# Self-attention of a Perceiver layer: projections and scores issued in groups of two head pairs, the loads around them rearranged

## Chip, cores, metric

The kernel runs on one core of a Trainium2 chip. Its time is the device time of one launch in microseconds (us), here the median of three runs of the kernel before. Beside it stands one execution that the hardware profiler recorded; all durations in this document that are not called the median come from that execution.

## Reference

One layer in fp32 on x, of shape (2, 256, 256), with a context of (2, 4096, 256). It has three parts, each added to x after a layer norm of x: cross-attention on the context, self-attention with 16 heads of 64 channels and 16 learnt memory keys ahead of the 256 token keys, and a gated FFN with quantised weights. The change touches self-attention alone:

```python
q = x @ Wq
k, v = jnp.split(x @ Wkv, 2, axis=-1)             # 16 heads of 64, memory keys and values ahead
dots = jnp.einsum('bhid,bhjd->bhij', q, k) * scale
dots = jnp.einsum('bhij,hk->bkij', dots, pre_proj)   # heads are mixed before the softmax
dots = jnp.where(causal, mask_value, dots)
attn = jax.nn.softmax(dots, axis=-1)
attn = jnp.einsum('bhij,hk->bkij', attn, post_proj)  # and after it
out = jnp.einsum('bhij,bhjd->bhid', attn, v)
out = out.transpose(0, 2, 1, 3).reshape(b, n, INNER) @ Wo
```

## The kernel before

Three functions follow one another, each a block that starts all engines together: cross-attention (to about 1103 us of the span), `self_attention` (to about 1290 us), and the FFN. Each engine runs its own list of instructions in order; semaphores tie them together, and every order in it is written out by hand.

`self_attention` begins with the layer norm of x. VectorE takes the statistics of four token tiles (`normalise_rows`, L56 and L60), GpSimd turns the variances into inverse deviations (`invert_std`, L71 to L75), VectorE scales (L64), TensorE transposes the result (L1249) and VectorE copies it to `xnT` (L1125). GpSimd has other work in the same stretch, ahead of `invert_std` in its list: it clears the padded `xnT` (L985) and makes the constants `spread` and `columns` (L986 to L995).

SyncE issues all loads of this part: the queries' weights (L963), the keys' and values' weights as one load of 2 MB (L964), the two mixing matrices (L965, L966), eight small loads of the memory keys (L968), three FFN weights (L769), the output weights (L972). After them it issues, with GpSimd, the regrouping of the scores (L956), copies from SBUF to SBUF that bring the heads of a row of queries together.

TensorE then projects. A projection (`project`, L1289) is two products of 128x128 weights with 512 columns, four matmul passes in fp32. The 26 projections are Q and K of pair 0, Q and K of pair 1, and so on for eight pairs of heads (n = 0 to 15), then ten for V (n = 16 to 25). Projection n writes one of four half banks (banks 2 and 3), and waits until projection n - 4 was copied out: even n by ScalarE (L1053), odd n by VectorE (L1020, L1024). Scores (`dots`, L1300) of a pair are four passes on 64 rows of the array, two for each head; step n of `dots` writes bank n % 2 and waits until step n - 2 was copied out (ScalarE L1056 for even n, VectorE L1166 for odd n). Steps 0 to 7 are the first 128 queries (144 keys), 8 to 15 the second 128 queries (272 keys) of batch item 0. The order is: projections 2m and 2m + 1, then dots m - 1, for m = 0 to 7; dots 7; then dots 8 + n and V projection n in turn, for n = 0 to 7; then the last two V projections. Between projections 2 and 3 TensorE makes the small constants (`small_constants`, L1257 and L1259: one product with `spread`, one transpose of the memory keys) and waits until VectorE copied them (L1135).

VectorE's copy of each odd projection is followed by one of six parts of the quantisation of an FFN weight (`quantise_weight`, L780 to L800); the first copy of a projection on VectorE waits for the three FFN weights (`hidden_in`). After the projections come the transposes of the FFN weights (L807), then the mixing steps (L1315), the softmax, the product with V and the output.

Of the kernel before, what the change touches and what calls it, by code (L numbers as in the profile page):

```python
# [12 lines left out]
P = 128  # L13
# [3 lines left out]
INNER = HEADS * DH  # L17
TOK_TILES = BATCH * SEQ // P
QT = SEQ // P
DC = D // P  # L20
PAIRS = HEADS // 2
# [47 lines left out]
def invert_std(pool, moments, power, chain, inverse_std):  # L69

    pool.memset(power[:, :], -0.5).then_inc(inverse_std, 1)  # L71
    pool.wait_ge(chain, 2 * TOK_TILES)
    pool.tensor_scalar(moments[:, :, 1], moments[:, :, 1], EPS, None, ALU.add).then_inc(inverse_std, 1)
    pool.wait_ge(inverse_std, 2)
    pool.tensor_tensor(moments[:, :, 1], moments[:, :, 1], power[:, :], ALU.pow).then_inc(inverse_std, 1)  # L75
# [665 lines left out]
MEM = 16  # L741
# [68 lines left out]
def self_attention(nc, w_q, w_kv, w_o, pre_proj, post_proj, mem_k, mem_v, w_gate, w_up, w_down, ffn_wT,  # L810
# [9 lines left out]
    with ExitStack() as stack:  # L820
        r = Resources(nc, stack)
# [21 lines left out]
        moments = r.sbuf("moments2", [P, TOK_TILES, 2])  # L843
# [24 lines left out]
        bank = [r.psum(f"bank{n}", [P, 2, 512]) for n in range(4)]  # L868

        wq_in = r.sem("wq_in")  # L870
        wkv_in = r.sem("wkv_in")
        wo_in = r.sem("wo_in")
        hidden_in = r.sem("hidden_in")
        hidden_chain = r.sem("hidden_chain")
# [39 lines left out]
        NQK = 2 * PAIRS  # L914
# [46 lines left out]
        @block.sync  # L961
        def _(sp):
            sp.dma_start(wq_sb, w_q.rearrange("(c p) n -> p c n", p=P)).then_inc(wq_in, 16)  # L963
            sp.dma_start(wkv_sb, w_kv.rearrange("(c p) n -> p c n", p=P)).then_inc(wkv_in, 16)  # L964
            sp.dma_start(proj_sb[:, 0, :], pre_proj).then_inc(small_in, 16)  # L965
            sp.dma_start(proj_sb[:, 1, :], post_proj).then_inc(small_in, 16)  # L966
            for pair in range(PAIRS):
                sp.dma_start(memk_sb[pair * MEM:(pair + 1) * MEM, :, :],  # L968
                             mem_k[2 * pair:2 * pair + 2].rearrange("h m d -> m h d")).then_inc(small_in, 16)
            for n, w in ((GATE, w_gate), (UP, w_up), (DOWN, w_down)):  # L970
                load_ffn_weight(sp, hidden_w[n], w, hidden_in)
            sp.dma_start(wo_sb[:, :, :], w_o.rearrange("(c p) n -> p c n", p=P)).then_inc(wo_in, 16)  # L972
            for b in range(BATCH):
                for t in range(QT):
                    regroup(sp, b, t, 0)
                if b == 0:
                    for eng in range(2):
                        sp.wait_ge(proj_copied[eng], NPROJ // 2)
                    for m in range(BATCH):
                        sp.dma_start(v_sb[0:MEM, m * QT, :].rearrange("m (h d) -> m h d", h=HEADS),  # L980
                                     mem_v.rearrange("h m d -> m h d")).then_inc(memv_in, 16)

        @block.gpsimd
        def _(pool):
            pool.memset(xnT[:, :, :], 0.0).then_inc(padded, 1)  # L985
            pool.memset(spread[:, :], 1.0).then_inc(consts, 1)  # L986
            for n in range(GPS):
                for c in range(STEP_ROWS):
                    pool.memset(columns[:, n, c:c + 1], float(c - n * ROWS)).then_inc(consts, 1)
            pool.wait_ge(consts, 1 + GPS * STEP_ROWS)  # L990

            pool.affine_select(out=spread[:, :], in_=spread[:, :], compare_op=ALU.is_ge, fill=0.0, base=0,
                               pattern=[[1, P]], channel_multiplier=-ROWS).then_inc(consts, 1)
            pool.wait_ge(consts, 2 + GPS * STEP_ROWS)
            pool.affine_select(out=spread[:, :], in_=spread[:, :], compare_op=ALU.is_ge, fill=0.0, base=ROWS - 1,  # L995
                               pattern=[[-1, P]], channel_multiplier=ROWS).then_inc(consts, 1)
            invert_std(pool, moments, power, norm_chain, inverse_std)

            for b in range(BATCH):
                if b > 0:  # L1000
                    for t in range(QT):
                        regroup(pool, b, t, 1)
                for s in range(RING):
                    n = b * SA_STEPS + s
                    if n >= RING:
                        pool.wait_ge(post_made, n - RING + 1)
                    pool.memset(expd[:, n % RING, :, step_keys(s):KEYS], 0.0).then_inc(tail_zero, 1)
                if b == 0:
                    for t in range(QT):
                        regroup(pool, b, t, 1)  # L1010
# [16 lines left out]
        def copy_dots(eng, scaled_copy, n):  # L1027
            t = n // PAIRS % QT
            pair = n % PAIRS
            keys = dot_keys(t)  # L1030
            eng.wait_ge(dots_made, n + 1)
            if n >= PAIRS:

                for half in range(2):
                    eng.wait_ge(regrouped[half][pair], 16 * (n // PAIRS))
            scaled_copy(dots_sb[:, 2 * pair:2 * pair + 2, 0:keys], bank[n % 2][:, :, 0:keys]
                        ).then_inc(dots_copied[n % 2], 1)
# [13 lines left out]
        def _(act):  # L1051
# [6 lines left out]
            def copy_projections(first, end):  # L1058
                for n in range(first, end, 2):
                    act.wait_ge(proj_made, n + 1)  # L1060
                    copy_projection(copy, n)
# [17 lines left out]
                for n in range((b * QT + t) * PAIRS, (b * QT + t + 1) * PAIRS, 2):  # L1079
                    copy_dots(act, scaled_copy, n)  # L1080

            for m in range(PAIRS):
                copy_projections(2 * m, 2 * m + 2)
                if m > 0 and (m - 1) % 2 == 0:
                    copy_dots(act, scaled_copy, m - 1)
            if (PAIRS - 1) % 2 == 0:
                copy_dots(act, scaled_copy, PAIRS - 1)
            for n in range(PAIRS, 2 * PAIRS):
                if n % 2 == 0:
                    copy_dots(act, scaled_copy, n)  # L1090
# [29 lines left out]
        def _(dve):  # L1120
# [84 lines left out]
                for n in range((b * QT + t) * PAIRS + 1, (b * QT + t + 1) * PAIRS, 2):  # L1205
                    copy_dots(dve, scaled_copy, n)

            for m in range(PAIRS):
                copy_projections(2 * m, 2 * m + 2)
                if m > 0 and (m - 1) % 2 == 1:  # L1210
                    copy_dots(dve, scaled_copy, m - 1)
            if (PAIRS - 1) % 2 == 1:
                copy_dots(dve, scaled_copy, PAIRS - 1)
            for n in range(PAIRS, 2 * PAIRS):
                if n % 2 == 1:
                    copy_dots(dve, scaled_copy, n)
# [27 lines left out]
        def _(pe):  # L1244
            mm = pe.matmul
            pe.wait_ge(norm_chain, NORMALISED)
            for c in range(DC):
                for t in range(TOK_TILES):
                    last = pe.transpose(bank[0][:, c, t * P:(t + 1) * P], xn[:, t, c * P:(c + 1) * P], ident[:, :])  # L1249
                last.then_inc(xT_made, 1)  # L1250
            pe.wait_ge(xT_copied, DC)
            pe.wait_ge(wq_in, 16)

            def small_constants():
                pe.wait_ge(small_in, 16 * (2 + PAIRS))
# [3 lines left out]
                pe.transpose(bank[1][:, 1, 0:P], memk_sb[:, :, :].rearrange("p a d -> p (a d)"), ident[:, :]  # L1259
                             ).then_inc(memk_made, 1)  # L1260

            def project(n):
                kind, m = projections[n]
                if n == 1:
                    pe.wait_ge(wkv_in, 16)
                if n == 3:
                    small_constants()
                    pe.wait_ge(memk_copied, BATCH)
                if n >= 4:
                    pe.wait_ge(proj_copied[n % 2], (n - 4) // 2 + 1)  # L1270
                for c in range(DC):
                    if kind == Q:
                        w, a = wq_sb[:, c, m * P:(m + 1) * P], xnT_tokens[:, c]
                    elif kind == K:
                        w, a = wkv_sb[:, c, m * P:(m + 1) * P], xnT_tokens[:, c]
                    else:
                        at = INNER + (m % 2) * 512
                        first = m // 2 // QT * PADDED + m // 2 % QT * P
                        a = wkv_sb[:, c, at:at + 512]
                        if m < 2 * TOK_TILES:  # L1280
                            w = xnT[:, c, first:first + P]
                        else:
                            w = [xnT[:, c, b * PADDED + QT * P:b * PADDED + QT * P + TAIL_ROWS] for b in range(BATCH)]
                    if kind == V and m >= 2 * TOK_TILES:
                        for b in range(BATCH):
                            last = mm(projection_bank(n)[b * TAIL_ROWS:(b + 1) * TAIL_ROWS], w[b], a,
                                      start=(c == 0), stop=(c == DC - 1))
                    else:
                        last = mm(projection_bank(n), w, a, start=(c == 0), stop=(c == DC - 1))  # L1289
                last.then_inc(proj_made, 1)  # L1290
# [71 lines left out]
            def dots_of_pair(m):  # L1362
                for eng in range(2):
                    pe.wait_ge(proj_copied[eng], m + 1)
                dots(m)

            for m in range(PAIRS):
                project(2 * m)
                project(2 * m + 1)
                if m > 0:  # L1370
                    dots_of_pair(m - 1)
            dots_of_pair(PAIRS - 1)
            for n in range(PAIRS):
                dots(PAIRS + n)
                project(NQK + n)
            for n in range(NQK + PAIRS, NPROJ):
                project(n)
            for eng in range(2):
# [378 lines left out]
```

## Time and profile before

| | us |
|---|---|
| median of 3 runs | 1374.15 (1373.31 to 1375.81) |
| the profiled execution | 1373.69 |
| its span | 1371.9 |
| TensorE busy | 1266.9 |
| VectorE busy | 865.2 |
| ScalarE busy | 880.6 |
| GpSimd busy | 411.3 |

The span is what the engines' records cover; 1.8 us of the execution's time lie around it. Times on the left of a row of the timeline are counted from the span's start. PE is the matmul engine (TensorE), PEld its weight loads, DVE VectorE, ACT ScalarE, POOL GpSimd, SP SyncE; a q behind an engine's name means its queue (sequencer), which issues DMAs. The time in brackets is how long the engine had been idle, with what ended it.

### The profile page before, as it was taken

How to read it: one execution, taken by the hardware profiler on the slowest of the kernel's cores; microseconds unless marked ns; L12 is line 12 of the kernel's file. 1: busy time of each engine (PE TensorE's matmuls, PEld its weight loads, DVE VectorE, ACT ScalarE, POOL GpSimd, SP SyncE). 2: the span in 40 equal slices, each digit the busy share in tenths (PEclk: the TensorE clock that was granted, in tenths of full speed). 3: DMA queues.
4: the chain of work that ended last, by engine and by line, in shares of the span. 5: the costliest groups of instructions: out<-in, count | busy, mean ns of one | idle time of the engine just before them, and what ended most of it. 6: DMA issues, size and time to landing. Idle time of an engine off the chain costs nothing. (4 is left out here: it accounts for less than half of the span.)

```text
span 1371.9 us, 21416 instructions
## 1 busy us (share of the span) xinstructions
PE 1266.9 (92%) x8447; PEld 1004.7 (73%) x8447; DVE 865.2 (63%) x1121; ACT 880.6 (64%) x1543; POOL 411.3 (30%) x373
## 2 busy tenths in 40 slices
PE   4999999999999999999999999999999969898663
PEld 3887887878787878697878787878887734667422
DVE  4547575766766576736766766576757645657366
ACT  5858586867777776766867777776868412535242
POOL 4506061524334342321524334242515022030000
PEclk9999999999999999999999999999999979998876
DMA  5000000000000011200000000000000063352000
GB/s 172 1 2 20 1 20 1 20 1 20 11 10 16 1 36 47 81 1 1 20 0 20 14 8 20 1 20 2 16 1 4 1 202 58 38 68 33 1 0 16
DMA packets 29683, 34.62 MB, mean 25 GB/s; under 512 B 3984, under 2 KB 26000, under 8 KB 29328
## 3 DMA queue, kind: packets, MB, share of 16 engines
q1 hardware_dynamic: 27536, 29.83, 8.4%
q0 software_dynamic: 2048, 3.43, 1.8%
q8 instruction: 68, 1.11, 0.4%
q14 instruction: 31, 0.25, 0.1%
HBM read 25.89 MB, written 0.52 MB: 19 GB/s over the span
## 5 line engine op out<-in xcount | busy, mean ns | idle before, releaser
L505 DVE TENSOR_TENSOR prob_sum<-prob_sum,probs 128x1024 f32<-128x1024 f32 x224 | 261.7, 1222 | 171.0 <-ACT probs L426 170.3
L341 POOL TENSOR_TENSOR k_split<-probs,k_split 64x512 fp32r<-64x512 f32 x128 | 164.5, 1285 | 359.0 <-ACT probs L388 357.5
L482 DVE TENSOR_REDUCE step_max<-scores_a 128x2 f32<-128x1024 f32 x128 | 156.7, 1224 | 96.7 <-PE scores_a L608 96.7
L343 POOL TENSOR_TENSOR k_split<-probs,k_split 64x512 fp32r<-64x512 f32 x128 | 164.6, 1286 | 9.6
L426 ACT ACTIVATE probs<-scores_a 128x1024 f32<-128x1024 f32 x98 | 100.5, 1026 | 93.8 <-PE scores_a L621 93.8
L482 DVE TENSOR_REDUCE step_max<-scores_b 128x2 f32<-128x1024 f32 x128 | 155.7, 1217 | 0.0
L426 ACT ACTIVATE probs<-scores_b 128x1024 f32<-128x1024 f32 x98 | 100.6, 1027 | 55.9 <-PE scores_b L621 55.9
L333 POOL TENSOR_TENSOR w_lo<-w_raw,w_hi 128x768 fp32r<-128x768 f32 x16 | 38.4, 2400 | 298.3 <-ACT w_hi L355 298.2
L632 PE MATMUL out_ps<-probs,v_far 128*64 128x256 f32 x1024 | 118.0, 382 | 0.0
L632 PE MATMUL out_ps<-probs,v_near 128*64 128x256 f32 x1024 | 118.0, 382 | 0.0
L620 PE MATMUL scores_a<-q_twice,k_split 128*128 128x256 f32 x392 | 100.3, 288 | 0.2 <-ACT probs L426 0.2
L620 PE MATMUL scores_b<-q_twice,k_split 128*128 128x256 f32 x392 | 99.8, 287 | 0.0
L621 PE MATMUL scores_b<-q_low_max,k_ones 128*128 128x256 f32 x392 | 98.0, 282 | 0.0
L621 PE MATMUL scores_a<-q_low_max,k_ones 128*128 128x256 f32 x392 | 97.8, 282 | 0.0
L632 PEld LDWEIGHTS out_ps<-probs,v_near 128*64 128x64 f32 x1024 | 70.5, 137 | 36.8 <-issue 0.4
L632 PEld LDWEIGHTS out_ps<-probs,v_far 128*64 128x64 f32 x1024 | 70.5, 137 | 36.6
L572 PE MATMUL k_both<-ctxT_lo,w_hi 128*128 128x512 f32 x256 | 90.3, 434 | 5.6 <-ACT probs L388 3.5
L608 PE MATMUL scores_b<-k_split,q_twice 128*128 128x512 f32 x256 | 84.8, 413 | 8.4 <-DVE step_max L482 6.9
L379 ACT ACTIVATE k_split<-k_both 64x512 fp32r<-64x512 f32 x128 | 75.4, 589 | 20.9 <-PE k_both L572 19.4
L426 ACT ACTIVATE probs<-k_both 128x1024 f32<-128x1024 f32 x60 | 61.6, 1026 | 39.5 <-PE k_both L621 39.5
L403 ACT ACTIVATE k_ones<-k_split 64x512 fp32r<-64x512 f32 x128 | 80.7, 631 | 2.8
L405 ACT ACTIVATE k_ones<-k_split 64x512 fp32r<-64x512 f32 x128 | 80.4, 628 | 3.1
(218 smaller groups left out, 2866.0 us busy)
## 6 DMA issues: line engine op xcount, KB each, us to landing
ctx_rows<-in_ctx_dram SPq DMA_DIRECT2D x10, 512.0 KB, 3.9
w_raw<-in_L_xattn_w_v_dram SPq DMA_DIRECT2D x14, 256.0 KB, 3.4
probs<-in_ctx_dram SPq DMA_DIRECT2D x6, 512.0 KB, 6.2
grouped<-dots_sb SPq DMA_DIRECT2D x16, 136.0 KB
grouped<-dots_sb POOLq DMA_DIRECT2D x16, 136.0 KB, 13.2
w_raw<-in_L_xattn_w_q_dram SPq DMA_DIRECT2D x16, 128.0 KB, 2.4
w_raw<-in_L_xattn_w_k_dram SPq DMA_DIRECT2D x16, 128.0 KB, 2.6
wo_pair<-in_L_xattn_w_o_dram SPq DMA_DIRECT2D x16, 128.0 KB, 2.1
```

Of the source, the lines that this page charges most:

```text
L341: pool.tensor_tensor(k_split[DH:P, A, keys], staged[0:DH], k_split[0:DH, A, keys].bitcast(F32), ALU.subtract).then_inc(k_low, 1)
L343: pool.tensor_tensor(k_split[0:DH, B, keys], staged[DH:P], k_split[DH:P, B, keys].bitcast(F32), ALU.subtract).then_inc(k_low, 1)
L403: act.activation(k_ones[0:DH, A, keys], k_split[0:DH, A, keys].bitcast(F32), ACT.Copy).then_inc(k_copied, 1)
L405: act.activation(k_ones[DH:P, B, keys], k_split[DH:P, B, keys].bitcast(F32), ACT.Copy).then_inc(k_copied, 1)
L426: act.activation(probs[:, j % 2, h, :], flat_scores[score_bank(b, i, 2 * j + h)], ACT.Exp, scale=SCALE).then_inc(exp_done, 1)
L482: dve.tensor_reduce(step_max[:, :, 1 - h, j - 1], scores[h][:, :, :], X, ALU.max).then_inc(max_done, 1)
L505: dve.tensor_tensor(prob_sum[:, h, :], prob_sum[:, h, :], probs[:, j % 2, h, :], ALU.add).then_inc(sum_done, 1)
L572: last = mm(k_ps[j % 2][:, :], w[:, c, 0:PAIR], s[:, c, j * CHUNK:(j + 1) * CHUNK], start=(n == 0), stop=(n == len(passes) - 1))
L608: last = mm(scores[h][:, qt, :], q_twice[:, h, qt * P:(qt + 1) * P], k_split[:, h, keys], start=True, stop=True)
L620: mm(out, k_split[:, h, keys], q_twice[:, h, :], start=True, stop=False)
L621: last = mm(out, k_ones[:, h, keys], q_low_max[:, h, :], start=False, stop=True)
L632: last = mm(out_ps[h * DH:(h + 1) * DH, SEQ:2 * SEQ], v[:, h * DH:(h + 1) * DH], probs[:, j % 2, h, t * SEQ:(t + 1) * SEQ], start=(j == 0 ...
```

## The change

The order of projections and dots goes from one pair at a time to two: four projections, then two dots. For the first half it is projections 0 to 3, 4 to 7, dots 0 and 1, projections 8 to 11, dots 2 and 3, projections 12 to 15, dots 4 and 5, dots 6 and 7; then dots 8 and 9, V projections 0 and 1, and so on. The copies on ScalarE and VectorE follow that order in the first half. The keys' and values' weights come as two loads of 1 MB on semaphores of their own. The ten small loads (mixing matrices, memory keys) are issued by ScalarE. GpSimd runs `invert_std` directly after clearing `xnT`. TensorE makes the small constants directly after the transposes of x, ahead of its waits for `xT_copied` and `wq_in`.

```diff
--- before.py
+++ after.py
@@ -868,7 +868,7 @@
         bank = [r.psum(f"bank{n}", [P, 2, 512]) for n in range(4)]
 
         wq_in = r.sem("wq_in")
-        wkv_in = r.sem("wkv_in")
+        wkv_in = [r.sem("wk_in"), r.sem("wv_in")]
         wo_in = r.sem("wo_in")
         hidden_in = r.sem("hidden_in")
         hidden_chain = r.sem("hidden_chain")
@@ -961,12 +961,10 @@
         @block.sync
         def _(sp):
             sp.dma_start(wq_sb, w_q.rearrange("(c p) n -> p c n", p=P)).then_inc(wq_in, 16)
-            sp.dma_start(wkv_sb, w_kv.rearrange("(c p) n -> p c n", p=P)).then_inc(wkv_in, 16)
-            sp.dma_start(proj_sb[:, 0, :], pre_proj).then_inc(small_in, 16)
-            sp.dma_start(proj_sb[:, 1, :], post_proj).then_inc(small_in, 16)
-            for pair in range(PAIRS):
-                sp.dma_start(memk_sb[pair * MEM:(pair + 1) * MEM, :, :],
-                             mem_k[2 * pair:2 * pair + 2].rearrange("h m d -> m h d")).then_inc(small_in, 16)
+            for part in range(2):
+                columns_of = slice(part * INNER, (part + 1) * INNER)
+                sp.dma_start(wkv_sb[:, :, columns_of], w_kv[:, columns_of].rearrange("(c p) n -> p c n", p=P)
+                             ).then_inc(wkv_in[part], 16)
             for n, w in ((GATE, w_gate), (UP, w_up), (DOWN, w_down)):
                 load_ffn_weight(sp, hidden_w[n], w, hidden_in)
             sp.dma_start(wo_sb[:, :, :], w_o.rearrange("(c p) n -> p c n", p=P)).then_inc(wo_in, 16)
@@ -983,6 +981,8 @@
         @block.gpsimd
         def _(pool):
             pool.memset(xnT[:, :, :], 0.0).then_inc(padded, 1)
+            invert_std(pool, moments, power, norm_chain, inverse_std)
+            pool.wait_ge(inverse_std, 3)
             pool.memset(spread[:, :], 1.0).then_inc(consts, 1)
             for n in range(GPS):
                 for c in range(STEP_ROWS):
@@ -994,7 +994,6 @@
             pool.wait_ge(consts, 2 + GPS * STEP_ROWS)
             pool.affine_select(out=spread[:, :], in_=spread[:, :], compare_op=ALU.is_ge, fill=0.0, base=ROWS - 1,
                                pattern=[[-1, P]], channel_multiplier=ROWS).then_inc(consts, 1)
-            invert_std(pool, moments, power, norm_chain, inverse_std)
 
             for b in range(BATCH):
                 if b > 0:
@@ -1079,12 +1078,16 @@
                 for n in range((b * QT + t) * PAIRS, (b * QT + t + 1) * PAIRS, 2):
                     copy_dots(act, scaled_copy, n)
 
-            for m in range(PAIRS):
-                copy_projections(2 * m, 2 * m + 2)
-                if m > 0 and (m - 1) % 2 == 0:
-                    copy_dots(act, scaled_copy, m - 1)
-            if (PAIRS - 1) % 2 == 0:
-                copy_dots(act, scaled_copy, PAIRS - 1)
+            act.dma_start(proj_sb[:, 0, :], pre_proj).then_inc(small_in, 16)
+            act.dma_start(proj_sb[:, 1, :], post_proj).then_inc(small_in, 16)
+            for pair in range(PAIRS):
+                act.dma_start(memk_sb[pair * MEM:(pair + 1) * MEM, :, :],
+                              mem_k[2 * pair:2 * pair + 2].rearrange("h m d -> m h d")).then_inc(small_in, 16)
+            for m in range(0, PAIRS, 2):
+                copy_projections(2 * m, 2 * m + 4)
+                if m > 0:
+                    copy_dots(act, scaled_copy, m - 2)
+            copy_dots(act, scaled_copy, PAIRS - 2)
             for n in range(PAIRS, 2 * PAIRS):
                 if n % 2 == 0:
                     copy_dots(act, scaled_copy, n)
@@ -1205,12 +1208,11 @@
                 for n in range((b * QT + t) * PAIRS + 1, (b * QT + t + 1) * PAIRS, 2):
                     copy_dots(dve, scaled_copy, n)
 
-            for m in range(PAIRS):
-                copy_projections(2 * m, 2 * m + 2)
-                if m > 0 and (m - 1) % 2 == 1:
+            for m in range(0, PAIRS, 2):
+                copy_projections(2 * m, 2 * m + 4)
+                if m > 0:
                     copy_dots(dve, scaled_copy, m - 1)
-            if (PAIRS - 1) % 2 == 1:
-                copy_dots(dve, scaled_copy, PAIRS - 1)
+            copy_dots(dve, scaled_copy, PAIRS - 1)
             for n in range(PAIRS, 2 * PAIRS):
                 if n % 2 == 1:
                     copy_dots(dve, scaled_copy, n)
@@ -1248,8 +1250,6 @@
                 for t in range(TOK_TILES):
                     last = pe.transpose(bank[0][:, c, t * P:(t + 1) * P], xn[:, t, c * P:(c + 1) * P], ident[:, :])
                 last.then_inc(xT_made, 1)
-            pe.wait_ge(xT_copied, DC)
-            pe.wait_ge(wq_in, 16)
 
             def small_constants():
                 pe.wait_ge(small_in, 16 * (2 + PAIRS))
@@ -1259,12 +1259,17 @@
                 pe.transpose(bank[1][:, 1, 0:P], memk_sb[:, :, :].rearrange("p a d -> p (a d)"), ident[:, :]
                              ).then_inc(memk_made, 1)
 
+            small_constants()
+            pe.wait_ge(xT_copied, DC)
+            pe.wait_ge(wq_in, 16)
+
             def project(n):
                 kind, m = projections[n]
                 if n == 1:
-                    pe.wait_ge(wkv_in, 16)
+                    pe.wait_ge(wkv_in[0], 16)
+                if n == NQK:
+                    pe.wait_ge(wkv_in[1], 16)
                 if n == 3:
-                    small_constants()
                     pe.wait_ge(memk_copied, BATCH)
                 if n >= 4:
                     pe.wait_ge(proj_copied[n % 2], (n - 4) // 2 + 1)
@@ -1364,15 +1369,19 @@
                     pe.wait_ge(proj_copied[eng], m + 1)
                 dots(m)
 
-            for m in range(PAIRS):
-                project(2 * m)
-                project(2 * m + 1)
+            for m in range(0, PAIRS, 2):
+                for n in range(2 * m, 2 * m + 4):
+                    project(n)
                 if m > 0:
+                    dots_of_pair(m - 2)
                     dots_of_pair(m - 1)
+            dots_of_pair(PAIRS - 2)
             dots_of_pair(PAIRS - 1)
-            for n in range(PAIRS):
+            for n in range(0, PAIRS, 2):
                 dots(PAIRS + n)
+                dots(PAIRS + n + 1)
                 project(NQK + n)
+                project(NQK + n + 1)
             for n in range(NQK + PAIRS, NPROJ):
                 project(n)
             for eng in range(2):
```

## Rows read from the trace of the kernel before

**Rows 1.** The page, busy time by engine.

```profile
PE 1266.9 (92%) x8447; PEld 1004.7 (73%) x8447; DVE 865.2 (63%) x1121; ACT 880.6 (64%) x1543; POOL 411.3 (30%) x373
```

**Rows 2.** Windows: sum; PE, PEld, DVE, ACT, POOL busy; granted clock, DMA share, GB/s.

```profile
1103.00:1110.00 7.00, 0.01 (x1) 0.02 (x1) 4.10 (x12) 0.00 (x0) 5.32 (x42) 0.50 0.80 300
...
1122.00:1148.00 26.00, 26.00 (x76) 11.02 (x76) 17.43 (x25) 7.46 (x9) 3.92 (x6) 1.00 0.18 46
```

**Rows 3.** Timeline from 1103 us, GpSimd and VectorE: start, duration, what.

```profile
1103.27 1.04 POOL L985 MEMSET xnT<- 128x1120 f32 x1 [42.55 <-POOLq L95]
...
1104.75 0.38 DVE L60 BATCH_NORM_AGGREGATE moments<-stats 128x2 f32<-128x6 f32 x4
...
1106.23 0.22 POOL L73 TENSOR_SCALAR moments<-moments 128x4 f32<-128x4 f32 x1
1106.53 1.05 POOL L75 TENSOR_TENSOR moments<-moments,power 128x4 f32<-128x4 f32 x1
...
1107.61 2.32 DVE L64 TENSOR_SCALAR normed<-x_res,moments 128x256 f32<-128x256 f32 x4 [2.48 <-POOL moments L75]
```

**Rows 4.** Timeline of PE, first projections and the small constants.

```profile
1109.98 1.97 PE L1249 MATMUL bank<-ident,normed 128*128 128x128 f32 x8 [7.73 <-DVE normed L64]
1112.74 7.99 PE L1289 MATMUL bank<-xnT,shared 128*128 128x512 f32 x12 [0.78 <-DVE xnT L1125]
1120.66 0.40 PE L1257 MATMUL bank<-proj_sb,spread 16*128 16x32 f32 x2
...
1121.91 1.98 PE L1289 MATMUL bank<-xnT,shared 128*128 128x512 f32 x4 [0.58 <-DVE kT L1135]
```

**Rows 5.** Timeline, projections and dots in turn, with two weight loads.

```profile
1127.90 0.52 PE L1300 MATMUL bank<-kT,q_sb 64*128 64x144 f32 x4
...
1129.31 0.19 PEld L1289 LDWEIGHTS bank<-xnT,shared 128*128 128x128 f32 x1 [0.24 <-issue]
...
1129.74 0.19 PEld L1289 LDWEIGHTS bank<-xnT,shared 128*128 128x128 f32 x1 [0.24 <-issue]
...
1131.98 0.52 PE L1300 MATMUL bank<-kT,q_sb 64*128 64x144 f32 x4
...
1152.00 0.73 PE L1300 MATMUL bank<-kT,q_sb 64*128 64x272 f32 x4
...
1154.58 0.73 PE L1300 MATMUL bank<-kT,q_sb 64*128 64x272 f32 x4
```

**Rows 6.** Timeline around dots 6, 7 and 8, PE and VectorE.

```profile
1148.28 0.52 PE L1300 MATMUL bank<-kT,q_sb 64*128 64x144 f32 x4
...
1149.00 1.74 DVE L782 TENSOR_REDUCE w_scales<-wide 128x48 f32<-128x1536 f32 x1
...
1150.09 1.99 PE L1289 MATMUL bank<-shared,xnT 128*128 128x512 f32 x4
...
1150.66 0.45 DVE L1166 TENSOR_SCALAR dots_sb<-bank 128x288 f32<-128x288 f32 x1
```

**Rows 7.** SyncE's issues on the timeline: start, time that issuing took.

```profile
1105.24 3.73 SPq L968 DMA_DIRECT2D memk_sb<-in_L_attn_mem_k_dram  x8
...
1110.11 3.44 SPq L769 DMA_DIRECT2D wide<-in_L_ffn_w_down_dram  x1
```

**Rows 8.** DMA issues by line: count, KB each, us from issue to landing.

```profile
wo_pair<-in_L_xattn_w_o_dram SPq DMA_DIRECT2D x16, 128.0 KB, 2.1
...
shared<-in_L_attn_Wkv_dram SPq DMA_DIRECT2D x1, 2048.0 KB, 10.2
...
wide<-in_L_ffn_w_down_dram SPq DMA_DIRECT2D x1, 768.0 KB, 12.2
memk_sb<-in_L_attn_mem_k_dram SPq DMA_DIRECT2D x8, 8.0 KB, 7.7
```

**Rows 9.** Windows in the first mixing steps, columns as in rows 2.

```profile
1178.00:1182.00 4.00, 2.53 (x20) 2.38 (x20) 2.69 (x15) 1.81 (x12) 0.00 (x0) 1.00 0.56 62
...
1182.80:1186.20 3.40, 3.40 (x18) 3.35 (x17) 2.46 (x12) 2.03 (x10) 0.00 (x0) 0.50 0.01 1
```

## The prediction

> **What bounds the kernel now.** The page comes first: TensorE is busy for 92% of the span [rows 1]. The change lies in the 70 us at the start of self-attention, so the windows of that stretch come next. They show two regimes. From 1103 to 1110 us TensorE has nothing to do and its clock is granted at 0.50 (1.2 GHz), while VectorE and GpSimd work on the layer norm; from 1122 to 1148 us TensorE is busy all the time at 1.00 (2.4 GHz) [rows 2]. So the first regime is a chain through VectorE and GpSimd, and in the second only work or turns taken from TensorE itself count. I then read the timeline for what ends each wait. VectorE is idle for 2.48 us before L64, and GpSimd's power (L75) ends it [rows 3]. TensorE is idle for 7.73 us before the transposes, ended by L64; for 0.78 us before the first projection, ended by the copy of xnT; and projection 3 starts only after the small constants were copied, ended by L1135 [rows 4]. Whatever comes later in the kernel waits for this stretch, since the mixing starts after the last projection; a microsecond saved here is a microsecond of the span.
>
> **Part 1: GpSimd's deviation first.** L73 needs VectorE's aggregates, done at 1104.75 + 0.38 = 1105.13, yet it starts at 1106.23, since the constants stand ahead of it in GpSimd's list [rows 3]. Afterwards only the clearing of xnT (to 1104.31) and one small memset are ahead, so L73 starts at about 1105.20: **1.03 us earlier**, and L75, L64 and the transposes with it. The constants move behind L75. They filled GpSimd from 1104.31 to 1106.23, 1.92 us; from about 1106.6 on they end at 1108.6. Who needs them is the small-constants product, now at 1110.9 (below): cover 2.3 us. Behind them GpSimd has memsets of expd and the regrouping, whose first piece waits for dots.
>
> **Part 2: small constants ahead of the wait for xT.** Now L1257 starts at 1120.66, and the next projection at 1121.91 [rows 4]. Without them it would start at 1120.66: **1.25 us off**. They move to the end of the transposes, where TensorE idles for 0.78 us anyway. L1257 alone takes 0.40 us and both less than 1.25 us; at the lower clock of that stretch they may stick out of the 0.78 us. Bounds: 0 and 0.5 us; I take 0.1, since the two lie nearer to 0.7 us than to 1.25. Net 1.15. The copy by VectorE, for which projection 3 waits, is then done about 8 us before it is asked for.
>
> **Part 3: fewer turns between projections and dots.** One projection pass starts every 0.43 us (1129.31 to 1129.74); a pair with its dots takes 1131.98 - 1127.90 = 4.08 us, eight passes 3.44, leaving 0.64 for dots of 144 keys. With 272 keys: 2.58 - 4 x 0.43 = 0.86 [rows 5]. Four passes of 272 columns at 0.43 x 272/512 would alone take 0.91, so the two heads must overlap on their halves of the array: 0.46 and 0.24 us for the two sizes. Both leave the same rest, **0.40 us, for turning from 128 rows to 64 and back**. Before, there are 14 such turns (dots 0 to 5 singly, 6 to 8 together, 9 to 15 singly); afterwards 6: {0,1}, {2,3}, {4 to 9}, {10,11}, {12,13}, {14,15}. 8 x 0.40 = **3.2 us off**. If a turn is paid per dots and not per change, nothing is saved; if all of the rest goes, 3.2. I take 3.2 as the two sizes agree on it.
>
> **Part 4: what the grouping adds in the middle.** Dots 4 to 9 now stand in a row, on two banks. Call T the end of projection 15. VectorE's list is: copy K of pair 7, then a part of the quantisation (L782), and only then the copy of dots 5. In the trace of before L782 starts 0.72 us after T = 1148.28 and takes 1.74, so the copy behind it starts at T + 2.38 and takes 0.45 [rows 6]. Dots 7 wait for that copy, to T + 2.9. Dots 9 need dots 7 copied (0.52 for their passes by the record of dots 6, 0.45 for the copy, and what signalling adds): T + 4.0, then 0.46 and 0.2 for turning back: V projection 0 at T + 4.65. Pure work is 4 x 0.24 + 2 x 0.46 + 0.40 = 2.28, so TensorE stalls for 2.37. Before, T to the first V projection is 1150.09 - 1148.28 = 1.81 [rows 6] against 1.34 of work, a stall of 0.47. **Net 1.9 us on**. Late next would be ScalarE's copy of dots 6, which is ready 1 us before anyone waits.
>
> **Edits at nothing, and their cover.** SyncE loses ten issues (eight took 3.73 us, 0.47 each [rows 7]) and gains one; the FFN loads start up to 4 us earlier, but bytes are the limit: the DMA share is 0.80 from 1103 to 1110 [rows 2]. The last FFN weight lands at 1110.11 + 12.2 = 1122.3 [rows 7, 8]. VectorE's first K copy waits for it, and TensorE asks for that copy (projection 5) at about 1123.0: up to 0.2 us of stall if it lands no earlier; I put 0. The keys' weights land no later than the 2 MB did, at about 1113.9, when projection 1 needs them two microseconds or more later; the values' weights are not used before 1148. ScalarE's ten issues end at 1103.3 + 10 x 0.47 = 1108.0, and its first copy comes after 1115. Their landing is the unknown cost.
>
> **When do the small loads land?** TensorE asks for them at the end of the transposes, 1111.95 - 1.03 = 1110.9. No load of before was issued by ScalarE. Lower bound: the short load nearest to it took 2.1 us [rows 8], 1108.0 + 2.1 = 1110.1. Upper bound: the same loads on SyncE's queue, behind 3 MB of weights, took 7.7 us [rows 8], 1115.7. I take the lower end, since the 7.7 us were spent behind transfers of the same queue, and the small loads now share it with none. The Trainium skill, page "DMA: Bandwidth & Descriptors", section "Queues, rings and completion order", says that an engine of the DMA serves its queues in turn, a packet at a time. By that rule they would land little after the lower end and the sum would stand; by the row of SyncE's queue it would come to 1.9 us slower. No row of before has two such queues under full load.
>
> **Sum:** -1.03 - 1.15 - 3.2 + 1.9 = -3.5 us. Against the profiled execution (1373.69) that is 1370.2; it lies 0.46 under the median of 1374.15, so the forecast is **1370.6**. Bounds: -4.9 (the middle stall half of what I work out, small terms at their better end) to -2.6.
>
> **Rivals.**
>
> **A. The small loads land late (slower).** The place is TensorE's wait ahead of the first projection. Each microsecond after 1110.9 is one on the span, and the 0.6 us of constants lose their cover. The gain is gone at 1110.9 + 2.9 = 1113.8, and slower by over 0.2% from about 1116.6. At the 7.7 us of rows 8 it is +1.9 (1376.0). If ScalarE's issue is held as SyncE's was for 3.44 us at L769 [rows 7], the last landing is 1108.0 + 3.44 + 7.7 = 1119.1, 8.2 us late: -3.5 + 8.2 + 0.6 = +5.3, **1379.4**. For it: small loads among saturated engines; against it: their own queue. The Trainium skill, page "DMA: Bandwidth & Descriptors", section "Queues, rings and completion order", adds that ScalarE's queue is not a descriptor generator of its own. By that rule a full backlog of SyncE's could hold the small ones; no row here shows it either way.
>
> **B. They land 1 to 3 us late.** Then the gain shrinks to 0.4 to 2 us: about **1372.7**.
>
> **C. The clock falls in the middle.** Part 4 leaves TensorE idle for some 2 us between sparse dots. In the first mixing steps, where it was busy for 2.53 of 4 us with short passes, the clock fell to 0.50 for 3.4 us afterwards [rows 9]. The same behind T would cost half of 3.4 us, 1.7: **1372.3**; twice that, 1374.0. Against it: the stall stands between two dense stretches.
>
> **D. The turns cost per dots.** Then part 3 is void: -0.3, **1373.9**. Against it: equal rests of two sizes.
>
> **Chances.** Forecast 0.45; A at over 0.2% slower 0.10; A short of that and B 0.18; C 0.22; D 0.05. 0.2% is 2.75 us, about what a measurement of this kernel can tell from no change. Faster by more: the forecast and a few of the others, 0.48; within: B, C, D and most of what A has left, 0.42; slower 0.10. The range runs from 1369.0 to 1375.5; it leaves out the worse half of A and little below.
>
> **What would show it.** L73 at about 1105.2 and L1249 at 1109.0; L1257 directly behind the transposes, and the first projection at 1111.8 (A, B: later, with an idle time before L1257); no gap before projection 3; four passes at 0.43 between turns and a pair of dots of 272 keys with its turn at 1.3 us; dots 7 starting 2.9 us after dots 4, behind L782 and L1166; granted clock 1.00 through that stretch (C: 0.50); mixing 3.5 us earlier. The forecast is wrong if the first projection starts later than at 1112.7, or if the period of two V projections with two dots stays at 5.15 us instead of 4.75.

## The result, and the profile after

The median of 20 runs is 1378.17 us, against 1374.49 us for the kernel before in as many runs: a ratio of 1.0024, with a 95% interval of 1.0014 to 1.0035. The change makes the kernel slower by some 3.3 us; I had forecast 3.5 us off. A second measurement of the same kernel gave 1.0010 (0.9994 to 1.0026). The second interval still includes no change, so the loss rests on the first measurement and on the stage below.

Spans alone mislead here. The profiled execution of the changed kernel has a span of 1376.8 us, 4.9 more than before, but 2.42 of them lie ahead of self-attention, in code that did not change: the stage starts at 1105.69 us instead of 1103.27. Over the fourteen profiled executions of this study that start lies anywhere between 1101.6 and 1106.5 us, for the kernel before at 1103.27 and 1104.67, for the changed one at 1105.69 and 1103.38. So I read the **stage** instead: from GpSimd's clearing of xnT to the first mixing pass, 74.97 us before (twice) and 77.39 us changed (76.60 in its second profile). Behind the stage the two traces run alike: 193.66 us to the end of the span before, 193.72 changed. This part too varies from one execution to the next, between 192.6 and 195.6 us over the fourteen (192.6 in the second profile of the kernel before). The stage's 2.4 us are what the change costs; the rest of the 3.3 lies within the interval.

The start of the stage, in the changed kernel's timeline (GpSimd, VectorE, TensorE, ScalarE's and SyncE's queues):

```profile
1105.69 1.04 POOL L983 MEMSET xnT<- 128x1120 f32 x1 [42.57 <-POOLq L95]
...
1106.61 4.35 ACTq L1084 DMA_DIRECT2D memk_sb<-in_L_attn_mem_k_dram  x8
...
1107.64 0.23 POOL L73 TENSOR_SCALAR moments<-moments 128x4 f32<-128x4 f32 x1 [0.87 <-DVE moments L60]
...
1109.03 3.53 DVE L64 TENSOR_SCALAR normed<-x_res,moments 128x256 f32<-128x256 f32 x4 [1.48 <-POOL moments L75]
1109.05 0.19 POOL L986 MEMSET spread<- 16x128 f32 x1
1109.20 1.21 POOL L989 MEMSET columns<- 128x1 f32 x32
1110.03 5.27 SPq L769 DMA_DIRECT2D wide<-in_L_ffn_w_down_dram  x1
...
1111.13 1.28 POOL L1006 MEMSET expd<- 128x480 f32 x3
...
1112.62 1.97 PE L1251 MATMUL bank<-ident,normed 128*128 128x128 f32 x8 [7.93 <-DVE normed L64]
...
1118.51 0.63 PE L1257 MATMUL bank<-proj_sb,spread 16*128 16x32 f32 x2 [3.92 <-DMA memk_sb<-in_L_attn_mem_k_dram]
1119.07 0.47 PE L1259 MATMUL bank<-ident,memk_sb 128*128 128x128 f32 x1
...
1119.34 10.95 PE L1294 MATMUL bank<-xnT,shared 128*128 128x512 f32 x20
```

Three things are to be seen, with the times of before in [rows 3, 4]. L73 runs 1.01 us earlier in the stage (1.95 instead of 2.96 us in), as forecast. L64 behind it takes 3.53 us instead of 2.32, with two runs of GpSimd's memsets beside it, the small ones of `columns` and then the three of expd, so that the transposes start 6.93 us in instead of 6.71: later, not earlier. And TensorE then stands for 3.92 us for the last load of the memory keys. The first projection starts 13.65 us in instead of 9.47: **4.18 us late**.

The middle of the stage, in PE's timeline of the changed kernel:

```profile
1150.87 0.76 PE L1305 MATMUL bank<-kT,q_sb 64*128 64x144 f32 x8
1151.99 0.52 PE L1305 MATMUL bank<-kT,q_sb 64*128 64x144 f32 x4 [0.36 <-ACT dots_sb L1055]
1153.84 2.34 PE L1305 MATMUL bank<-kT,q_sb 64*128 64x144 f32 x12 [1.33 <-DVE dots_sb L1169]
1156.12 4.57 PE L1294 MATMUL bank<-shared,xnT 128*128 128x512 f32 x8
1160.61 1.19 PE L1305 MATMUL bank<-kT,q_sb 64*128 64x272 f32 x8
...
1165.36 1.19 PE L1305 MATMUL bank<-kT,q_sb 64*128 64x272 f32 x8
```

and its windows (columns as in rows 2):

```profile
1151.00:1154.70 3.70, 2.01 (x20) 1.33 (x20) 3.00 (x4) 0.82 (x2) 1.31 (x3) 0.97 0.21 40
...
1154.50:1157.85 3.35, 3.35 (x10) 1.34 (x7) 1.08 (x2) 0.62 (x1) 2.45 (x5) 0.50 0.70 104
1157.95:1160.00 2.05, 2.05 (x6) 0.94 (x5) 0.00 (x0) 0.60 (x1) 0.00 (x0) 1.00 0.66 73
```

Dots 4 start at T = 1150.87, dots 7 at T + 2.97 (forecast 2.9), the first V projection at T + 5.25 (forecast 4.65). The clock fell to 0.50 for 3.4 us behind the stall: rival C happened as well. Two V projections with two dots take 1165.36 - 1160.61 = 4.75 us, as forecast.

### The profile page after: what moved, and what is told of

The parts are those of the page before. It is cut to its first block and busy times, and to the rows that moved or that the text cites. A ratio compares the mean times of both kernels' runs of the same rounds, so it can differ in the third digit from the quotient of the medians.

```text
span 1376.8 us, 21418 instructions
## 1 busy us (share of the span) xinstructions
PE 1267.8 (92%) x8447; PEld 1010.6 (73%) x8447; DVE 866.5 (63%) x1121; ACT 879.8 (64%) x1543; POOL 411.5 (30%) x373
```

## The experiments

Names with b_ are the kernel before with one part of the change; names with a_ are the changed kernel with one part undone. In the table, transposes and first projection are starts in us into the stage; the last two columns are lengths in us.

| kernel | ratio to before (95%) | transposes | first projection | first projection to last two V | stage |
|---|---|---|---|---|---|
| before | 1 | 6.71 | 9.47 | 57.28 | 74.97 |
| changed | 1.0024 (1.0014 to 1.0035) | 6.93 | 13.65 | 55.52 | 77.39 |
| changed, again | 1.0010 (0.9994 to 1.0026) | 6.93 | 12.10 | 56.28 | 76.60 |
| a_consts_back | 1.0001 (0.9987 to 1.0015) | 6.93 | 9.68 | 56.13 | 74.03 |
| a_sp_waits | 1.0025 (1.0011 to 1.0039) | 6.93 | 9.68 | 58.91 | 76.81 |
| b_act_loads | 1.0006 (0.9992 to 1.0019) | 6.73 | 9.48 | 57.10 | 74.80 |
| b_dev_first | 0.9989 (0.9978 to 1.0001) | 6.93 | 9.68 | 56.21 | 74.11 |
| b_dev_quiet | 0.9992 (0.9979 to 1.0006) | 4.78 | 7.53 | 58.32 | 74.07 |
| b_consts_late | 1.0000 (0.9987 to 1.0014) | 6.72 | 9.47 | 56.58 | 74.28 |
| b_group | 0.9986 (0.9975 to 0.9997) | 6.73 | 9.48 | 56.79 | 74.50 |
| b_group_mid | 0.9984 (0.9971 to 0.9997) | 6.73 | 9.48 | 54.22 | 71.92 |
| best1 | 0.9963 (0.9949 to 0.9978) | 4.78 | 7.53 | 54.46 | 70.21 |
| best2 | 0.9954 (0.9938 to 0.9970) | 4.77 | 7.52 | 54.01 | 69.75 |

One caution on the last two columns: the clock rises from 0.50 to 1.00 between 3.1 and 5.5 us after the first projection (5.2 before), and differs in this also between kernels that do the same there. A microsecond earlier is half a microsecond of stage, so a stage length is good to about 1 us. The starts ahead of it repeat to 0.02 us where no load is awaited.

**The early wait for the small loads: a_consts_back.**

```diff
-            small_constants()
             pe.wait_ge(xT_copied, DC)
...
                 if n == 3:
+                    small_constants()
                     pe.wait_ge(memk_copied, BATCH)
```

> The changed kernel with the small constants back between projections 2 and 3. Stage time is counted from the clearing of xnT to the first mixing pass: 74.97 us before, 77.39 changed. If the early wait for the small loads is the cause (theory 1), the first projection starts about 9.7 us into the stage instead of 13.65, the 1.3 us gap at projection 3 is back, and the stage takes 77.39 - 4.0 + 1.3 - 0.8 (constants no longer ahead) = about 74.0. If the order in groups or the middle stall costs the time (theory 2), the stage stays near 77.

The first projection starts 9.68 us in, and the stage takes 74.03: theory 1. The stage is 3.4 us shorter than the changed kernel's, and the measured loss is gone (1.0001). Not all of the 3.4 is the place of that one wait. The start is 3.97 us earlier and the gap at projection 3 is back, at 1.25 us, which leaves 2.7 for the wait. The rest is the clock, which did not fall in the middle here (some 1.5) and rose 1.0 us later behind the first projection (0.5 the other way). The three make 3.7, good to the 1 us said above. What is left against before is 0.22 us on for L64 and 1.3 off by parts 3 and 4: 73.9 by the sum.

**Why the loads come late: b_act_loads and a_sp_waits.** The first moves the ten loads to ScalarE in the kernel before and nothing else.

> The kernel before with the ten small loads issued by ScalarE and nothing else. They landed 12.8 us into the stage in the changed kernel. If two queues under full load are the cause, they land at about the same time here (12 to 13 us), no engine waits for them (asked for at 17.4 us), and the stage stays at 75.0, or 74.8 if the FFN weights land earlier. If they landed late because of something else in the change, they land at about 7 us.

The second holds SyncE's queue back in the changed kernel:

```diff
             sp.dma_start(wq_sb, ...).then_inc(wq_in, 16)
+            sp.wait_ge(small_in, 16 * (2 + PAIRS))
             for part in range(2):
```

> The changed kernel, but SyncE issues the keys' and all later weights only after the small loads have landed, so that the small loads share the DMA engines with 1 MB alone. If the backlog of SyncE's queue makes them late, they land about 2 us after the last issue, 7.3 to 7.5 us into the stage, and the first projection starts at about 9.8 instead of 13.65. If ScalarE's issues are slow by themselves, they land later than 10. The FFN weights land 2 us later (about 21), which may stall projection 5: stage 74 to 76.

The DMA issues of the memory keys (the last figure of a row is the median time from issue to landing), first of the changed kernel:

```profile
memk_sb<-in_L_attn_mem_k_dram ACTq DMA_DIRECT2D x8, 8.0 KB, 6.3
```

then of a_sp_waits:

```profile
memk_sb<-in_L_attn_mem_k_dram ACTq DMA_DIRECT2D x8, 8.0 KB, 3.3
```

A load of 8 KB on ScalarE's queue lands after 6.3 us beside SyncE's backlog and after 3.3 us with only the queries' weights in flight; the latest of the eight took 8.0 and 4.3. SyncE could go on 7.07 us into the stage, so the small loads had landed by then instead of at 12.8, and the first projection came at 9.68. In b_act_loads the eight took 6.3 to 7.2 us with the other parts of the change absent. So it is the backlog, and not the position of ScalarE's issues or anything else in the change. Where between issue and landing the small loads are held, no run here separates. The price of the cure was as high as the illness: the FFN weights came later, TensorE stood 0.40 us for the keys' weights and 2.70 us for the first K copy, the clock fell behind that gap, and the kernel is as slow as the changed one (1.0025).

The Trainium skill says in "DMA: Bandwidth & Descriptors", section "Issuing engines are not separate DMA queues", that issuing from several engines saves no more than the sequencer's time for issuing. The runs agree in the main: on SyncE's queue the eight took 7.7 us to land [rows 8], on ScalarE's 6.3, and not the 2.1 that I had hoped for from a queue of their own.

**GpSimd beside VectorE: b_dev_first and b_dev_quiet.** Both put `invert_std` first in the kernel before; they differ in one wait of GpSimd ahead of the constants:

```diff
             invert_std(pool, moments, power, norm_chain, inverse_std)
-            pool.wait_ge(inverse_std, 3)
+            pool.wait_ge(norm_chain, NORMALISED)
             pool.memset(spread[:, :], 1.0).then_inc(consts, 1)
```

> The kernel before with the deviation first on GpSimd and nothing else. My forecast was 1.03 us off. Theory 3, from the changed kernel's trace (L64 3.53 us instead of 2.32, with GpSimd's small memsets beside it): the power ends 1.0 us earlier, but L64 takes about 3.5 us, and the transposes start 0.2 us later; stage 75.0 to 75.2. If the longer L64 has another cause (the loads of ScalarE), L64 stays at 2.3 and the stage takes 74.0.

> As b_dev_first, but GpSimd starts the constants only when L64 is done. Theory 3: L64 takes 4 x 0.4 = 1.6 us, the transposes start 5.0 us into the stage instead of 6.71, the stage takes about 73.3. If GpSimd's work beside L64 is not what makes it long, L64 takes 2.3 to 3.5 us as in b_dev_first.

L64 in the two, by its line (durations of one in ns: shortest, median, longest); first b_dev_first:

```profile
L64 DVE TENSOR_SCALAR normed<-x_res,moments x4: 396/867/1641, 1106.8 to 1108.7; 128x256 f32<-128x256 f32 x4
```

then two of its four one by one, the first and the last:

```profile
L64 DVE TENSOR_SCALAR normed<-x_res,moments x1: 1332/1332/1332, 1106.8 to 1106.8; 128x256 f32<-128x256 f32 x1
...
L64 DVE TENSOR_SCALAR normed<-x_res,moments x1: 1641/1641/1641, 1108.7 to 1108.7; 128x256 f32<-128x256 f32 x1
```

GpSimd beside them, in the same execution:

```profile
1107.00 1.21 POOL L991 MEMSET columns<- 128x1 f32 x32
...
1108.93 1.28 POOL L1008 MEMSET expd<- 128x480 f32 x3
```

and L64 in b_dev_quiet:

```profile
L64 DVE TENSOR_SCALAR normed<-x_res,moments x4: 408/409/413, 1109.1 to 1110.1; 128x256 f32<-128x256 f32 x4
```

Each of the four takes 0.41 us when GpSimd is silent. In b_dev_first the first takes 1.33 us and is done at about 1108.2, as the 32 memsets of 128x1 end; the next two take 0.40 each, beside two selects on 16 partitions; the last takes 1.64 us, and ends at 1110.36, 0.15 us behind the three memsets of expd. So two of the four are held, each until a whole run of memsets is over. The row of before (2.32 us in all, [rows 3]) was itself a contended one: there the first alone is held, for 1.36 us beside expd's memsets, and the other three take 0.40. The 1.21 us more are a second run beside L64, the small memsets that moved (0.9), and 0.3 more beside expd's. Silence brings the transposes 1.93 us forward, from 6.71 to 4.78. The ScalarE loads have no part in it: with them alone, in b_act_loads, L64 takes 2.32 us. A kernel with the small memsets alone beside L64 was not tried. The Trainium skill says in "SBUF — State Buffer", section "Who interferes with whom", that VectorE in its two-port mode and GpSimd hold a port pair for a whole instruction and exclude one another. The trace agrees with the exclusion, though none of these runs shows the mode of L64; but one of expd's memsets lasts 0.44 to 0.49 us and a small one 0.10, and the instructions beside them lost 1.23 and 0.92 us, so each lost more than one turn.

b_dev_first has its transposes 0.22 us late, as theory 3 had it; its stage is a microsecond shorter than expected all the same, since the clock rose 3.1 us after the first projection there instead of 5.2.

In b_dev_quiet the 1.93 us did not reach the end of the stage: it takes 74.07. PE's timeline of b_dev_quiet at the first dots, and VectorE's:

```profile
1121.95 1.98 PE L1290 MATMUL bank<-xnT,shared 128*128 128x512 f32 x4 [0.58 <-DVE kT L1136]
1125.46 0.52 PE L1301 MATMUL bank<-kT,q_sb 64*128 64x144 f32 x4 [1.52 <-DVE kT L1021]
```

```profile
1124.62 0.69 DVE L1021 COPY kT<-bank 128x512 f32<-128x512 f32 x1 [1.77 <-DMA wide<-in_L_ffn_w_down_dram]
```

VectorE stands in front of its first copy of K for the last FFN weight, and TensorE behind it for 1.52 us. The weights land some 19 us into the stage, whatever starts earlier; they are next in line.

**The constants without the wait for their copy: b_consts_late.** The wait for `memk_copied` moves from projection 3 to the first dots.

> The kernel before, with the small constants still ahead of projection 3, but the wait for their copy only at the first dots. If the wait for the copy is a good part of the 1.25 us of part 2, projection 3 starts 0.6 us sooner behind L1257 and the stage loses 0.6; if the FFN weights (19 us into the stage) bind behind it, the gain appears as a wait for the K copy and the stage stays at 74.5 to 75.

Projection 3 follows L1257 after 0.51 us instead of 1.25, so 0.74 of the 1.25 us was waiting. PE's timeline:

```profile
1118.51 0.40 PE L1257 MATMUL bank<-proj_sb,spread 16*128 16x32 f32 x2
1118.84 0.34 PE L1259 MATMUL bank<-ident,memk_sb 128*128 128x128 f32 x1
1119.02 1.88 PE L1288 MATMUL bank<-xnT,shared 128*128 128x512 f32 x4
1121.62 0.52 PE L1299 MATMUL bank<-kT,q_sb 64*128 64x144 f32 x4 [0.73 <-DVE kT L1020]
```

The next wait takes it back: 0.73 us ahead of the first dots, for VectorE's first copy of K. That copy starts 19.0 us into the stage, where the last FFN weight lands. The ratio of 1.0000 says so too. The stage of 74.28 is 0.7 shorter because the clock rose 1.3 us earlier.

**The grouping: b_group and b_group_mid.** b_group has the order and the copies of the change and nothing else. b_group_mid lets VectorE copy dots 5, 7 and 9 ahead of a part of the quantisation (the loops that copied them later leave them out, which is not shown):

```diff
                     copy_projection(dve.tensor_copy, n)
+                    if dots_between and n == NQK - 1:
+                        copy_dots(dve, scaled_copy, PAIRS - 3)
+                        copy_dots(dve, scaled_copy, PAIRS - 1)
+                        copy_dots(dve, scaled_copy, PAIRS + 1)
                     m, part = n // 2 // W_PARTS, n // 2 % W_PARTS
```

> The kernel before with the grouping alone. By parts 3 and 4 of the prediction: 3.2 us off, 1.9 us on in the middle, stage 73.6; with a fall of the clock in the middle as in the changed kernel (granted 0.50 for 2.9 us) up to 1.5 more, 75.1. If turns are paid per dots (rival D), 76.9.

> Grouping alone, and VectorE copies dots 5, 7 and 9 directly after the last K, ahead of the part of the quantisation. If that part is what stalls the middle, dots 7 start 1.3 us after dots 4 instead of 2.97, the first V projection 3.1 us after them instead of 5.25, the clock stays at 1.00, and the stage is 2 to 3 us shorter than b_group.

b_group is faster than before (0.9986). Its stage, 74.50, lies between the forecast with and without a fall of the clock, and the clock did fall, for 3.4 us, which the eight passes behind the stall show (5.40 us instead of 3.70); against that it rose 1.9 us earlier behind the first projection, worth 0.9. PE's timeline of b_group_mid in the middle:

```profile
1149.09 0.76 PE L1302 MATMUL bank<-kT,q_sb 64*128 64x144 f32 x8
1150.21 0.81 PE L1302 MATMUL bank<-kT,q_sb 64*128 64x144 f32 x8 [0.36 <-ACT dots_sb L1056]
1151.23 1.19 PE L1302 MATMUL bank<-kT,q_sb 64*128 64x272 f32 x8 [0.20 <-ACT dots_sb L1056]
1152.34 3.70 PE L1291 MATMUL bank<-shared,xnT 128*128 128x512 f32 x8
```

The V projections start 3.25 us after dots 4, instead of 4.70 in b_group and 5.25 in the changed kernel; the first eight of their passes take 3.70 us instead of 5.40 and 4.57, and the clock stays at 1.00. From the first projection to the last two V the kernel needs 54.22 us instead of 57.28, 3.06 off. The sum of it: 3.2 us of part 3, less 0.5, since the middle still stalls for 3.25 - 2.28 = 0.97 us instead of 0.47, and 0.4 for a clock that rose 4.5 us after the first projection instead of 5.2. The total agrees within its interval: 0.9984 is 2.2 us (0.4 to 4.0).

**Together: best1 and best2.** best1 is b_dev_quiet, b_group_mid and b_consts_late in one, with all loads on SyncE's queue as before. best2 also moves the wait for the FFN weights:

```diff
-            dve.wait_ge(hidden_in, 48)
...
                     copy_projection(dve.tensor_copy, n)
+                    if n == 1:
+                        dve.wait_ge(hidden_in, 48)
```

> All that is expected to help: deviation first with the constants after L64 (1.7 us off), grouping with the dots' copies ahead of the quantisation (3 to 4 off), small constants made ahead of projection 3 with the wait for their copy only at the first dots (0.7 off); loads as before on SyncE. Stage 69 to 70 us, time about 1369.

> best1, but VectorE waits for the FFN weights behind its first copy of K instead of ahead of it. In best1 and b_dev_quiet the earlier start ran into the landing of the last FFN weight, 19 us into the stage (TensorE idle 1.52 us for the K copy in b_dev_quiet). If that is what kept b_dev_quiet from its full gain, no such gap is left and the stage takes 68.5 to 69.2 us instead of 70.21; if another wait ends there, it stays at 70.

best1 gave 1369.61 us, 0.9963; best2 1368.81 us, 0.9954, or 6.3 us less than before. In best2 no idle time stands between the first projection and the first dots any more; its stage of 69.75 missed the 69.2 that I expected, with no new wait to be seen there. The step from best1 to best2 is 0.46 us of stage. The clock rises at nearly the same point in both (5.5 and 5.4 us after the first projection), and the twenty passes ahead of the first dots take 9.16 us in best1 and 8.75 in best2. In best1 VectorE still waited there, 1.35 us, for the last FFN weight. So the traces, one of each, show that wait at 0.4 us. The totals can't tell the two kernels apart; that both beat before and changed they show.

**Both kernels once more: a_again and b_again.**

> The changed kernel once more, for how far its stretches repeat. Expected: small loads landed 12.5 to 13 us into the stage, first projection at 13.3 to 13.9, dots 7 at 3.0 us behind dots 4; stage 76 to 78, as the clock's rise and its fall in the middle shift by up to 2 us.

> The kernel before once more. Expected: first projection 9.47 us into the stage, stage 74 to 75.5. The start of the stage moves with the cross-attention ahead of it, which took 1103.27 us before and 1105.69 in the changed kernel: if that difference is chance and none of the change's, this run starts anywhere between 1101 and 1107.

The kernel before repeats in the starts of the table to 0.02 us. The changed kernel does not: TensorE waited 2.37 us for the loads instead of 3.92, and started projecting at 12.10 instead of 13.65, which is below the 13.3 that I had expected at least. So this wait on loads among saturated engines differed by 1.5 us between two executions. The clock fell in the middle again.

## Why the prediction was wrong

**Part 1 (1.03 off) failed in its last link.** L73 and L75 came earlier as worked out. I moved L64 along with them at its 2.32 us, and costed the constants behind L75 by asking only who needs them (cover 2.3 us), not what runs beside them. Beside them ran L64, at 3.53 us, since the moved memsets held its first instruction for 0.9 us and expd's still held its last. The transposes were 0.22 us later instead of 1.03 earlier (b_dev_first alone gives the same 0.22).

**The landing of the small loads (taken at 1110.1) is the step that turned the sign.** I put it at the lower end, by loads of 128 KB (2.1 us in the median) from a stretch without such a backlog, and took the 7.7 us of SyncE's queue for the effect of a shared queue. They landed at about 1105.69 + 12.8, which counted from the old start is 1116.1: my upper end was 1115.7, and rival A the right case, at a chance of 0.28 in its two forms with B. The landing alone would have stayed just short of rival A's 1116.6 for a loss of over 0.2%; L64 and the clock made up the rest. Its mechanism, ScalarE's issue held, was at most a small part: the eight issues took 4.35 us instead of 3.73. The rule of taking turns that I cited from the Trainium skill ("DMA: Bandwidth & Descriptors", "Queues, rings and completion order") did not give the early landing that I read into it.

**Part 2 (1.15 off)** did take away the gap: the projections run from 0 to 7 without one. It was paid for with the wait above. Where the loads had landed, in a_sp_waits, the two products fit ahead of the first projection at no cost (it starts 2.75 us after the transposes start, 2.76 before), so the 0.1 that I put for them was 0. And 0.74 of its 1.25 us can be had without moving the constants, as b_consts_late shows, though another wait takes it back there.

**Part 3 (3.2 off) was right,** in its 0.40 us for a turn, in its count of 8 turns, and in its size: it is what the 3.06 us of b_group_mid need. Rival D is refuted by the period of 4.75 us.

**Part 4 (1.9 on) was right:** in a_consts_back, whose clock did not fall, V starts 4.70 us behind dots 4, against 4.65 worked out. The changed kernel adds rival C to it: V begins 0.6 us later than that, and eight passes that take 3.70 at 1.00 take 4.57, together some 1.5 us. The clock fell there in three (changed, its repeat, b_group) of the five profiles that have this stall, and in none of the three without it. I gave it 0.22.

**The sum** with the measured terms, for the profiled execution: 4.18 for the start of the projections (0.22 of it L64, 3.96 the wait and the constants that lost their cover), -1.25, -3.2 + 1.9, +1.5 for the clock's fall, and -0.4 because the clock rose 4.4 us after the first projection instead of 5.2: +2.7 against +2.42 measured. 0.3 us stay unexplained. Two of my terms hold, two were wrong in the same direction, and the two wrong ones are 5 us.

## What to carry to other kernels

A load that is moved to another queue is not moved off the DMA engines: its landing is read from what is in flight at that time, and the wait on it goes where a late landing costs nothing. Work that moves on GpSimd must be read against what VectorE does in its new place, not only against who needs its result. And where a grouping puts several steps on two buffers in a row, the list of the engine that empties them decides whether the gain arrives; here moving three copies ahead of a piece of quantisation took 1.45 us of stall out of the middle (4.70 to 3.25 us), and the clock did not fall behind it.

## What was not expected of the hardware

Four VectorE instructions of 0.41 us each (128x256, fp32) took 1.38 us with GpSimd silent, 2.32 beside one run of GpSimd's memsets (three of 416 to 480 columns), and 3.53 beside two runs (32 of one column, then the three); each run held one of the four until it was over. A load of 8 KB took 6.1 to 8.0 us beside another queue's backlog, though its own queue held nothing but small loads. And the granted clock fell to 0.50 after a stretch in which TensorE was busy for 2.01 of 3.70 us, although dense work stood on both sides of it; in two other profiles with the same stall (a_consts_back, a_sp_waits), with TensorE busy for the same 2.01 of 3.70 us, it did not fall, and what decides between them these runs leave open.
